# Border head's blocks and strips moved ahead of the batch seam; row sum, variance, logits and third query in another order

## The reference

```python
q, k, v = x @ wq, x @ wk, x @ wv              # k and v are shared by 4 query heads each
x = _layernorm(x + causal_attention(q, k, v) @ wo)
logits = clip(x @ gate_w.T, -50, 50)           # 8 experts
top_w, top_idx = top_k(logits, 2)
rw = softmax(top_w)
x = _layernorm(x + x @ W.T + sparse_part_of_chosen_experts(x, rw, top_idx))
```

## Time and profile before

| | us |
|---|---|
| median of 3 runs | 1853.06 (1845.52 to 1854.03) |
| the profiled execution | 1849.14 |
| its span | 1847.3 |
| TensorE busy (PE) | 1732.2 (94%) |
| VectorE busy (DVE) | 1297.7 (70%) |
| GpSimd busy (POOL) | 843.3 (46%) |
| ScalarE busy (ACT) | 810.6 (44%) |

### The profile page before, as it was taken

The page is one execution under the profiler, slowest core; times in us unless marked ns, Lnnn a source line. Parts: engine busy times, 40 slices in busy tenths (PEclk is TensorE's granted clock), DMA queues, the critical chain, the costliest instruction groups (busy, mean ns, idle before and its releaser), DMA issues.

```text
span 1847.3 us, 33274 instructions
## 1 busy us (share of the span) xinstructions
PE 1732.2 (94%) x8750; PEld 1450.6 (79%) x8750; DVE 1297.7 (70%) x4027; ACT 810.6 (44%) x1950; POOL 843.3 (46%) x1221
## 2 busy tenths in 40 slices
PE   8999999998999899999999999989998999989983
PEld 7888878887888788877887788878887778777772
DVE  5566568866887688768886788678867876662356
ACT  4444344434443444534553445444543443333454
POOL 6775355534554244333334333343333333665564
PEclk9999999999999999999999999999999999999997
DMA  9655455655555766666665676566666558444698
GB/s 327 233 213 197 171 186 186 185 163 200 172 173 166 236 206 205 200 218 207 229 217 180 187 226 230 196 191 231 209 208 224 175 168 326 144 149 143 225 334 329
DMA packets 195148, 386.41 MB, mean 209 GB/s; under 512 B 27328, under 2 KB 98144, under 8 KB 184480
## 3 DMA queue, kind: packets, MB, share of 16 engines
q1 hardware_dynamic: 176688, 344.53, 54.9%
q0 software_dynamic: 18288, 39.80, 6.8%
HBM read 261.64 MB, written 122.62 MB: 208 GB/s over the span
## 4 chain that ended last, share of the span: by engine, by line
PE 66%; DVE 13%; issue 9%; DMA 5%; ACT 3%; POOL 2%; SPq 1%; DVEq 1%; another core or an unknown queue 0%; ACTq 0%; POOLq 0%
PE psum L1607 19%; PE psum L1609 18%; PE psum L1608 18%; PE psum L1635 4%; PE psum L2488 2%; PE psum L2490 2%; PE psum L2489 2%; DVE pT_lo L2064 2%; DMA probs_strips<-probs_blocks 1%; DVE probs_blocks L2076 1%; DVE route_product L700 1%; DVE probs L2053 1%; DMA probs_moved<-probs_strips 1%; DMA token_rows<-x,ids_now 1%; PE psum L376 1%
## 5 line engine op out<-in xcount | busy, mean ns | idle before, releaser
L1471 POOL TENSOR_SCALAR probs<-probs,row_inv 128x128 f32<-128x128 f32 (+3 forms) x512 | 295.4, 602 | 432.3 <-DVE row_inv L2061 431.1
L1913 ACT ACTIVATE probs<-probs,neg_max 128x512 f32<-128x512 f32 (+3 forms) x512 | 281.7, 553 | 192.4 <-DVE neg_max L2053 191.8
L1607 PE MATMUL psum<-xT_hi,w_hi 128*128 128x512 f32 x640 | 256.8, 401 | 16.3 <-DVE oT_lo L2064 16.0
L1609 PE MATMUL psum<-xT_hi,w_lo 128*128 128x512 f32 x640 | 251.5, 393 | 0.0
L1608 PE MATMUL psum<-xT_lo,w_hi 128*128 128x512 f32 x640 | 250.9, 392 | 0.0
L1935 ACT ACTIVATE qT_hi<-psum 128x512 fp32r<-128x512 f32 x128 | 76.7, 600 | 388.1 <-PE psum L1609 383.7
L2053 DVE CUSTOM_DVE_ANT_0 probs<-psum,causal 128x512 f32<-128x512 f32 (+3 forms) x512 | 220.8, 485 | 27.7 <-issue 16.0
L1607 PE MATMUL psum<-wo_hi,oT_hi 128*128 128x512 f32 x496 | 199.2, 402 | 16.4 <-DVE y_acc L2111 9.4
L1609 PE MATMUL psum<-wo_hi,oT_lo 128*128 128x512 f32 x496 | 194.2, 392 | 0.0
L1608 PE MATMUL psum<-wo_lo,oT_hi 128*128 128x512 f32 x496 | 193.9, 391 | 0.0
L1607 PE MATMUL psum<-kT_hi,qT_hi 128*128 128x512 f32 (+3 forms) x512 | 166.4, 325 | 1.5 <-DVE qT_lo L2097 1.3
(11 more groups left out here) (255 smaller groups left out, 4101.5 us busy)
## 6 DMA issues: line engine op xcount, KB each, us to landing
w_hi<-split_qk_weights SPq DMA_DIRECT2D x140, 256.0 KB, 5.7
w_lo<-split_qk_weights SPq DMA_DIRECT2D x140, 256.0 KB, 6.8
probs_strips<-probs_blocks SPq DMA_DIRECT2D x54, 640.0 KB
probs_moved<-probs_strips SPq DMA_DIRECT2D x216, 160.0 KB
wo_hi<-split_out_weights SPq DMA_DIRECT2D x27, 1024.0 KB
wo_lo<-split_out_weights SPq DMA_DIRECT2D x27, 1024.0 KB
expert_weights_hi_lo<-split_expert_weights SPq DMA_DIRECT2D x8, 2048.0 KB, 9.5
x_in<-in_L_attn_x_dram SPq DMA_DIRECT2D x8, 1024.0 KB, 6.0
```

The lines of the kernel that those rows point to most:

```text
L1471: last = pool.tensor_scalar(p, p, row_inv[:, buf, i:i + 1], 1.0, ALU.mult, ALU.mult)
L1607: pe.matmul(dst, hi_s, hi_m, start=start, stop=False)
L1609: return pe.matmul(dst, lo_s, hi_m, start=False, stop=stop)
L1913: last = act.activation(probs[:, buf, a:a + w], probs[:, buf, a:a + w], ACT.Exp, bias=neg_max[:, buf, i:i + 1], scale=-1.0, accum_out=row_ ...
```

## The change

Six edits, all in the order of the work; no instruction of TensorE or GpSimd moves.

1. *Blocks and strips of the border head.* For k = 0 of a first group, `turn_blocks` and `move` go to the end of the batch before: VectorE's blocks stand between the ranks and the addition of row 2, SyncE's strips and moves ahead of the store of the residual.
2. *Output weights.* In a first group `fetch_wo` goes from the group's start to behind `move` of k = 1; in the others it stays there.
3. *Third query and exponentials.* In the groups behind the first, ScalarE runs the exponentials of head n+1 ahead of qT_hi of n+2, and VectorE the reciprocal of the row sum (`inverse`) ahead of qT_lo; the blocks come last.
4. *Variance.* There, the variance goes from ahead of the addition of row 1 to behind the maxima of n+2, and the normalization from ahead of the addition of row 2 to behind pT_lo of n+1.
5. *Logits.* In a first group kT_lo comes behind the first logit product and the first oT_lo behind the second; the rest comes later. In a "group" kT_lo and oT_lo come one logit product earlier.
6. *Best experts.* In a first group `route_best` comes behind qT_lo of n+4 instead of ahead of it.

```diff
@@ SyncE, iteration
-            if is_moved(kind, route):
+            if is_moved(kind, route) and kind != "first":
                 move(it, 0, 3 * n)
...
-            if route and kind == "first":
-                fetch_wo(it, g)
             slot(3, it + 1, after)
...
             if is_moved(kind, route):
                 move(it, 1, 3 * (n + 2) + 3)
+            if route and kind != "end":
+                fetch_wo(it, g)
...
-            if route and kind not in ("first", "end"):
-                fetch_wo(it, g)
...
             if kind == "batch":
+                move(it + 1, 0, 3 * (n + G))
@@ ScalarE, iteration
-            if moved:
+            if kind == "first" and moved:
                 qT(n + 2, 0, BANK_A)
             exps(n + 1, 1)
+            if kind != "first" and moved:
+                qT(n + 2, 0, BANK_A)
@@ VectorE, iteration
             if moved:
+                if kind != "first":
+                    inverse(n + 1, 1)
                 qT(n + 2, 0, BANK_A)
-                turn_blocks(n, it, 0)
-                inverse(n + 1, 1)
+                if kind != "first":
+                    turn_blocks(n, it, 0)
+                else:
+                    inverse(n + 1, 1)
...
-            if early:
+            if early and not moved:
                 route_variance(dve, R, tt)
...
                 maxima(n + 2, 0)
+                if early:
+                    route_variance(dve, R, tt)
...
-            if early and kind != "end":
-                route_normalize(dve, R, tt)
...
             pT(n, 1, moved)
             if early and moved:
+                route_normalize(dve, R, tt)
                 route_logits(dve, R, tt, (0,), products)
...
             if late and moved:
                 route_normalize(dve, R, tt)
-                route_logits(dve, R, tt, (0, 1, 2), products)
+                route_logits(dve, R, tt, (0,), products)
+                kT(it + 1)
+                route_logits(dve, R, tt, (1,), products)
...
-            if key_first:
+            if key_first and not late:
                 kT(it + 1)
             oT(n, 0, 0, banks)
...
-            if route:
+            if route and not late:
                 route_best(dve, R, tt)
             if kind != "end":
                 qT(n + 4, 0, bank_of_query(0, banks))
+            if late:
+                route_best(dve, R, tt)
...
+                if kind == "batch":
+                    turn_blocks(n + G, it + 1, 0)
                 add_rows(it, 2, kind)
```

More of the change, by code:

```diff
@@ L2231, in iteration @@
                 route_normalize(dve, R, tt)
-                route_logits(dve, R, tt, (0, 1, 2), products)
-            if route and kind != "batch":
-                route_logits(dve, R, tt, (4,) if early else (3,), products)
+                route_logits(dve, R, tt, (0,), products)
+                kT(it + 1)
+                route_logits(dve, R, tt, (1,), products)
+            if early and kind != "batch":
+                route_logits(dve, R, tt, (4,), products)
             for q in quads[1:2]:
@@ L2237, in iteration @@
             inverse(n + 3, 1)
-            if route and kind != "batch":
-                route_logits(dve, R, tt, (5,) if early else (4, 5), products)
+            if kind == "end":
+                route_logits(dve, R, tt, (5,), products)
             for q in quads[1:2]:
                 count_later(dve, N, upper, q)
-            if key_first:
+            if key_first and not late:
                 kT(it + 1)
@@ L2247, in iteration @@
             if route:
-                route_logits(dve, R, tt, (3,) if kind == "batch" else (6,), products)
+                route_logits(dve, R, tt, {"first": (2,), "group": (5,), "batch": (3,), "end": (6,)}[kind], products)
             for q in quads[2:3]:
@@ L2259, in iteration @@
             if route:
-                route_logits(dve, R, tt, (6, 7) if kind == "batch" else (7,), products)
+                route_logits(dve, R, tt, {"first": range(3, NE), "group": (6, 7), "batch": (6, 7), "end": (7,)}[kind], products)
             for q in quads[2:3]:
```

## The result

The changed kernel took 1863.13 us (median of 10 runs, 1857.2 to 1866.62), the kernel before beside it 1849.08 us (10 runs, 1841.53 to 1854.03). The ratio is 1.0072, with a 95% interval of 1.0057 to 1.0088: slower by 13 us. The time lies in the range that was predicted, but 8 us above the predicted time and on the side that had a chance of 0.17. Against the kernel before beside it the miss is larger: +1.6 us were forecast and 13 measured, since that kernel's median came out 4 us lower than the one that the forecast starts from. The profiled execution took 1858.65 us, its span 1856.9 us, 9.6 us more than the span before.

A forecast was written before the change was run, and what follows sets the result against it. TensorE, busy 94% of the span, was taken to bound the kernel, so only its waits could be won. Terms +6.3 + 0 - 1.3 - 3.4 = +1.6 us on the median 1853.06 gave 1854.7 us; range 1837 to 1865 us.

The forecast's parts named there:

- the side that had a chance of 0.17: Whole kernel: slower than the kernel before by more than 0.5%; chance 0.17.
- Part 1, the seam: Between batches: border head's transposes ahead of the last additions delay the four jumps back; +6.3 us, bounds 0 and +16.
- the idle time moves with the jump: At the seams: VectorE's 3.28 us idle time shifts with the later jump, moving maxima, qT_lo and scores; within the +6.3 us.
- 0.8 + 0.7 predicted: Scattering loop's jump back: 0.8 us from the delayed addition, 0.7 us from two more maxima behind a second idle stretch.
- the second stretch: VectorE's 2.35 us idle among the scattering loop's border maxima: should fall after the first maximum, its end staying; 0.7 us.
- Part 2, the first groups: First groups: wait for oT_lo goes, wait for pT_lo grows equally; 0 in six, -1.3 us in the last batch.
- -1.3: Last batch's first group: TensorE keeps 1.3 us of its 3.2 us wait; bounds 0 and -3.2 us.
- Part 3, the other groups: Groups behind the first: wait ahead of row 2's output product goes, partly given back; -3.4 us, bounds +5 and -13.
- -1.8: Two scattering batches: chain has slack except in group 1; four groups keep 0.5 us, two lose 0.1; -1.8 us.
- an opponent: Scattering groups: normalization beside GpSimd's is slowed by up to 0.7 us each, making the sum 2 us higher.
- The waits did not stay gone: Rival, first and other groups: TensorE keeps all it gains from the removed waits; 1835.3 us, chance 0.19.
- wo was never late: Rival, first groups: wo lands 2 to 3 us late in each of seven; 1872 us, chance 0.12.

The follow-up runs named there:

- seam_only: Kernel before with only the border head's blocks and strips and the load of wo moved as in the change; ratio 1.0043.
- combo2_seam: Changed kernel with first groups' second strips ahead of the residual store, best and chosen experts behind qT_lo of n+5, normalization ahead of row 2's addition; ratio 0.9861.
- filler: Changed kernel with twelve unread products on TensorE in the wait ahead of each first group's second value product; ratio 1.0043.
- first_only: Kernel before with only the first group's VectorE order changed (kT_lo, oT_lo ahead of logits, best experts behind qT_lo); ratio 1.0063.
- norm_back: Changed kernel with the normalization of the groups behind the first put back ahead of the addition of row 2; ratio 1.0072.
- groups_only: Kernel before with only the groups behind the first reordered (exponentials, reciprocal, variance, normalization), logits, kT_lo and oT_lo as before; ratio 1.0015.
- strips_first: Changed kernel with each first group's second strips on SyncE ahead of the store of the residual row; ratio 0.9935.

## Why the prediction was right where it was, and where it failed

**Part 1, the seam: the amount right, its reason not shown.** +6.3 us were predicted, 5.1 measured, and 5.0 us of idle time with these edits alone. The sum took it that the idle time moves with the jump. In this kernel it did, by and large: the stretch was 3.28, 4.25 and 3.58 us behind the three later jumps and is 3.20, 3.16 and 3.11 us now, and 3.20 us in seam_only and combo2_seam. But in filler VectorE runs 1.4 us ahead at two of the jumps, and that brought nothing. At the seam shown above its last addition starts 1.6 us after TensorE's first scores of the batch (792.59), where the changed kernel has 3.0 us (799.98 after 797.01); its first maximum starts 6.9 us after them in both, and TensorE loses the same 1.7 us:

```profile
794.17 0.68 DVE L2116 TENSOR_TENSOR y_acc<-psum,y_acc 128x512 f32<-128x512 f32 x1
799.50 0.69 DVE L2058 CUSTOM_DVE_ANT_0 probs<-psum,causal 128x512 f32<-128x512 f32 x1 [4.64 <-issue]
```

The kernel before has the same: against TensorE's scores the addition ahead of its stretch of 4.25 us ended 1.0 us sooner than the one ahead of 3.28 us, and the maxima started within 0.1 us of each other. In filler the DMA engines are full until shortly before, and then a packet of the kind instruction shows (in 797.38 to 797.48), 2 us ahead of VectorE's first maximum:

```profile
796.00:797.00 1.00, 0.00 (x0) 1.00 1.00 379
797.00:798.00 1.00, 0.00 (x0) 1.00 0.15 50
```

```profile
q14 instruction: 1, 0.01, 19.3%
```

Edit 1 puts the strips' 640 KB ahead of that packet; at the 379 GB/s of this row they take 1.7 us (an estimate), as much as the transposes. So the loss may be owed to the strips and not to the transposes. No kernel here moves one without the other, and the cause stays open. Too much was the first jump: 0.8 + 0.7 predicted, 0.4 measured, because the second stretch shrank from 2.35 to 1.71 us. The Trainium skill (Runtime: NRT & Kernel Launch, Instruction fetch mechanics) says that a taken branch to a block that isn't held forces a fetch first, and the trace agrees, with a cost at each of the four jumps. By its second half the crossing into the next block in a straight run is mostly hidden; the 1.71 us, one maximum further on without a jump, were not.

**Part 2, the first groups: the waits right, their price wrong.** The step that failed is "So TensorE comes 1.7 us earlier and waits 1.7 us longer: 0". The wait for oT_lo went, the wait for pT_lo grew by as much and a little more (1.5 us over seven batches), and the chain behind SyncE stood still, all as written. But one wait of 3.1 to 4.2 us is not worth the same as one of 1.5 and one of 1.9 us with 9 us of work between them: behind it TensorE's clock was down, in seven batches of seven, which cost 1.5 to 2.4 us each, 13.3 us in all; in the kernel before in four, 6.2 us in all. The sum had no term for the clock, though the profile of before had such stretches, one of them in the very group of the earlier trace rows. first_only shows that these edits alone bring it, filler that work in the wait takes it away. In the last batch the value product did start 1.7 us sooner, and the slow stretch, which lay ahead of it before, now lay in it and took that back: 0 in place of -1.3.

**Part 3, the other groups: -3.4 predicted, -0.5 measured.** The waits ahead of row 2 went as predicted. In the splitting batches and the last one the sum was -3.9 us against the -1.6 foretold for them. In the two scattering batches it was +3.4 against -1.8: there TensorE got two new waits a group, for qT_lo and for oT_lo. "In the two scattering batches the chain has slack except in group 1" was wrong. What VectorE did ahead of the addition it now does behind it, and in those groups it has no spare time before oT_lo; with the normalization moved or not, TensorE waits (norm_back). That the normalization would be slower beside GpSimd was rightly named as an opponent and wrongly sized: it took 1.62 to 1.77 us in place of 0.55 in six groups and 0.73 in the others, where up to 0.7 more was allowed. The Trainium skill (SBUF — State Buffer, Who interferes with whom) has the two engines contend for a shared port pair, and these numbers agree with it in direction. Still only 1.4 us of the time hang on it.

**The rivals.** The waits did not stay gone. wo was never late: TensorE has no wait for it. The time came out on the slow side, but not by that rival's way, so the 0.12 that it held was not knowledge of the clock. That the time still lies in the stated range is luck in part: nothing in the range stood for the clock, and the kernel before came out 4 us lower than its base. With the clock priced as it was measured (13.3 us less 6.2) the sum would have been +8.7 us in place of +1.6.

## What to carry to other kernels

When an edit takes one wait away and another one behind it grows, ask whether they merge: a wait that becomes longer can cost more than the sum of two short ones, as here, where the matmuls behind each merged wait ran at the lower clock. Price a wait with the granted clock of the windows behind it, not by the list of waits. And before reordering an engine's work, look at the queue that the last wait hangs on: here the data were ready 7.5 us before SyncE sent them, behind a store that they had nothing to do with, and one moved call gave 0.9% where six edits had cost 0.7%.

## What the runs showed of the hardware

Over the seven kernels whose first groups still had a wait ahead of the second value product (before, changed, seam_only, first_only, groups_only, norm_back, strips_first), a wait of 3.0 to 4.3 us was followed by matmuls at the lower clock in 21 of 21 cases; one of 1.5 to 2.4 us in 7 of 24; one of 2.8 us, not; and in filler, with 0.6 to 1.4 us left, in 0 of 7. The last batch's 3.2 us ahead of the next query was followed by one in all three kernels of these that kept it (before, seam_only, groups_only). That the shorter ones differ from batch to batch may be part of why this kernel varies by some us from run to run; no run tests it, and what decides between them is open. GpSimd's products with row_inv went with a slower logit product too, and not with a slower normalization alone: it took 0.69 us alone, and 1.06 and 1.39 us beside them. And a jump back that VectorE reached 1.0 or 1.4 us sooner did not end its idle stretch sooner (before, filler).
